# The first normalization of a four-layer graph network in ten parts, and its constants loaded later

## The chip, the core and the metric

The kernel runs on one core of a Trainium2 chip. The core has a matrix engine (PE, TensorE), a vector engine (DVE), a scalar engine (ACT), GpSimd (POOL), and SyncE (SP), which here only issues transfers. Sixteen DMA engines move the data. The metric is the device time of one execution in microseconds (us), lower is better.

## What is computed

A residual stack of four graph layers over 4096 nodes with 128 features, on one dense 4096 x 4096 matrix `adj` in fp32:

```python
h = maximum(layernorm(x), 0);  x = x + (A/deg) @ h @ W_in + (A.T/deg_t) @ h @ W_out
h = maximum(layernorm(x), 0);  x = x + silu(A @ silu(A @ h @ W1 + b1) @ W1 + b1)
h = maximum(layernorm(x), 0);  x = x + relu(normalized(A + I) @ h @ W2 + b2)
h = maximum(layernorm(x), 0);  x = x + relu(normalized(A + I) @ (h @ W3) + b3)
```

`deg` and `deg_t` are the row sums of A and of its transpose. The change touches the first `layernorm` alone, with the loading of `x`, of the five weights and of the three biases.

## The kernel before

**Tiles.** `adj` and its transpose (both laid out by the host) come in tiles of 128 x 1024 fp32, 512 KB each, 768 in all; the code calls a tile's turn a substep. Tiles 0 to 255 are the first layer's; tile n goes through four steps, each on an engine of its own:

- SP loads it (`load(n)`, L316) into one of ten buffers `raw`. From tile 10 on the load waits until DVE is done with tile n - 10 (L320).
- ACT copies it, rounded to the type fp32r (`hi(n)`, L374), with row sums on the side. From tile 8 on this waits until PE has used tile n - 8: the rounded tiles stand in a ring of eight places, six in `a_hi`/`a_lo` and two, for tiles 6, 7, 14, 15, 22, 23 and so on, in the idle feature buffers `h_hi1`/`h_lo1`. So the rows of these tiles read `h_hi` where the others read `a_hi`, and one can tell which tile a row belongs to.
- DVE subtracts, which gives the rest (`lo(n)`, L515).
- PE does six matmuls of 512 columns (`products`, L732): rounded tile times `h_hi` and times `h_lo` of its block of features (L737, four matmuls), rest times `h_hi` (L741, two). The first four need the rounded tile and the features, the last two the rest as well.

**The first normalization.** The features are 32 blocks of 128 nodes. Before the change they are normalized in eight parts of four blocks. A part takes these steps: DVE takes statistics (`first_stats`, L522 and L526), ACT the square root (`first_std`, L388), DVE the reciprocal and bias (`first_affine`, L532 and L534), ACT four relus (`first_relu`, L407) and the rounding to `h_hi` (`split_hi`, L398), and DVE the rest `h_lo` (`split_lo`, L540). Part 0 stands at the start. The others stand among the tiles: the tables FIRST_STATS and so on (L282 to L286) name after which tile each step of which part is issued.

**Which tile needs which features.** Tiles 0 to 47 use blocks 0 to 7 over and over (six runs of eight tiles). From tile 48 on, 16 tiles use blocks 0 to 7, 16 use blocks 8 to 15, and so on; so block 8 is first needed by tile 64, block 16 by tile 80, block 24 by tile 96, block 28 by tile 100. PE waits for `h_ready` at every fourth block (L810). After each run ACT copies two banks out (`copy_partial`, L426), seven and eight tiles after the run's end.

**What follows.** After tile 111 the first block column is complete. PE multiplies it by the weights (L758, eight small matmuls in two rows of 128 columns each, the first after tile 113); this is the first use of a weight, and it waits for all eight loads of weights and biases. ACT's last two copies of the step, behind tile 118, wait in turn for these products.

**SP's order.** x's first eighth (256 KB), tile 0, x's second eighth, tiles 1 to 9, x's second quarter (512 KB), five weights and three biases (64 KB each; a bias is read once for every partition), then tiles from 10 on, with x's third quarter after tile 16 and its last after tile 32.

Of the kernel before, what the change touches and what calls it, by code (L numbers as in the profile page):

```python
# [5 lines left out]
F32 = mybir.dt.float32  # L6
F32R = mybir.dt.float32r
ALU = mybir.AluOpType
# [7 lines left out]
def build_gnn_stack(nc, x, adj, adj_t, w_in, w_out, w1, b1, w2, b2, w3, b3, out):  # L16
# [22 lines left out]
    with ctx:  # L39
# [181 lines left out]


        def split_n(sweep, q):
            return (sweep + 1) * NQ + q

# [55 lines left out]

        FIRST_STATS = {0: 1, 6: 2, 19: 3, 32: 4, 45: 5, 58: 6, 71: 7}  # L282
        FIRST_STD = {0: 1, 10: 2, 23: 3, 36: 4, 49: 5, 62: 6, 75: 7}
        FIRST_AFFINE = {0: 1, 11: 2, 24: 3, 37: 4, 50: 5, 63: 6, 76: 7}
        FIRST_RELU = {1: 1, 14: 2, 27: 3, 40: 4, 53: 5, 66: 6, 79: 7}
        FIRST_LO = {1: 1, 15: 2, 28: 3, 41: 4, 54: 5, 67: 6, 80: 7}  # L286

# [7 lines left out]
        def done1(at, i):  # L295
            return [q for q in range(NQ - 2) if START1 + SLOT1 * q + at == i]

        def halves(at, s):
# [11 lines left out]
        def _(sp):  # L310
# [17 lines left out]
            for n in range(1, RAWS):  # L328
                load(n)
            load_x(2)  # L330
            for i, w in enumerate((w_in, w_out, w1, w2, w3)):
                sp.dma_start(w_sb[:, i, :], w).then_inc(const_in, 16)  # L332
            for i, b in enumerate((b1, b2, b3)):
                sp.dma_start(b_sb[:, i, :], b.rearrange("(a n) -> a n", a=1).to_broadcast([P, D])).then_inc(const_in, 16)

            for n in range(RAWS, len(substeps)):
                load(n)
                if n in (16, 32):
                    load_x(2 + n // 16)

# [29 lines left out]
        def _(act):  # L370
# [13 lines left out]

            def first_std(q):
                blocks = slice(GB * q, GB * q + GB)
                act.wait_ge(mv0_ready, q + 1)
                act.activation(std0[:, blocks], mv0[:, blocks, 1], ACT.Sqrt, bias=eps_sb[:, 0:1]).then_inc(std0_ready, 1)  # L388
# [11 lines left out]

            def first_relu(q):
                act.wait_ge(bias0_ready, q + 1)
                if q > 0:
                    act.wait_ge(h_ready, split_n(-1, q))
                for b in range(GB):
                    n = GB * q + b
                    last = act.activation(act_raw[:, b * D:(b + 1) * D], x_sb[:, n, :], ACT.Relu,  # L407
                                          bias=bias0[:, n:n + 1], scale=rstd0[:, n:n + 1])
                last.then_inc(act_ready, 1)
                split_hi(-1, q)  # L410

# [46 lines left out]

            first_std(0)
            for n in range(S0):  # L460
                _, kind, d, k, _, _ = seq[n]
                hi(n, (row_part if kind else col_part)[:, k, d:d + 1])
                if n == 0:
                    first_relu(0)
                first_layer(n)
# [37 lines left out]
        def _(dve):  # L503
# [13 lines left out]

            def first_stats(q):
                blocks = range(GB * q, GB * q + GB)
                dve.wait_ge(x_in[q if q < 2 else q // 2 + 1], 16)  # L520
                for b in blocks:
                    last = dve.bn_stats(stats0[:, b, :], x_sb[:, b, :])  # L522
                last.then_inc(stats0_ready, 1)
                dve.wait_ge(stats0_ready, q + 1)
                for b in blocks:
                    last = dve.bn_aggr(mv0[:, b, :], stats0[:, b, :])  # L526
                last.then_inc(mv0_ready, 1)

            def first_affine(q):
                blocks = slice(GB * q, GB * q + GB)  # L530
                dve.wait_ge(std0_ready, q + 1)
                dve.reciprocal(rstd0[:, blocks], std0[:, blocks]).then_inc(rstd0_ready, 1)  # L532
                dve.wait_ge(rstd0_ready, q + 1)
                dve.scalar_tensor_tensor(out=bias0[:, blocks], in0=mv0[:, blocks, 0], scalar=-1.0, in1=rstd0[:, blocks],  # L534
                                         op0=ALU.mult, op1=ALU.mult).then_inc(bias0_ready, 1)

            def split_lo(sweep, q):
# [108 lines left out]
            def first_layer(n):  # L646
                if n in FIRST_LO:
                    split_lo(-1, FIRST_LO[n])
                if n in FIRST_STATS:
# [27 lines left out]

            first_stats(0)
            first_affine(0)
            for n in range(S0):  # L680
                lo(n)
                if n == 0:
                    split_lo(-1, 0)
                first_layer(n)
# [45 lines left out]
        def _(pe):  # L730
# [71 lines left out]
            for n in range(S0):  # L802
                r, _, _, k, first, last = seq[n]
                if first and r >= 3:
                    copied, added = drained(r - 3)
                    pe.wait_ge(part_copied, copied)
                    if added:
                        pe.wait_ge(part_added, added)
                if n <= step_end[0] and k % GB == 0:
                    pe.wait_ge(h_ready, k // GB + 1)  # L810
                products(n, h_hi[0][:, k, :], h_lo[0][:, k, :], run_ps[r % 3], first, last)
                first_layer(n)
# [77 lines left out]
```

## Time and profile before

| | |
|---|---|
| median of 3 runs | 1126.58 us (1125.49 to 1129.52) |
| the profiled execution | 1127.55 us, its span 1125.8 us |
| PE busy | 1106.7 us, 98% of the span |
| DVE, ACT busy | 93%, 81% |
| DMA | 363 GB/s on the mean, 95.5% of the 16 engines' time |

The page sums over the whole span. What the change touches is the first tenth, so the rows further down are taken from stretches of it. Times are from the start of the span. A row of the timeline gives start, duration, engine, line, what is written and read and how often; in brackets stands how long the engine was idle before it, and what ended that.

### The profile page before, as it was taken

To read this page: it belongs to the slowest core of one execution; us is meant where nothing else is said; L and a number is where in the kernel's file an instruction comes from. 1 tells how busy PE (TensorE), PEld (TensorE's weight loads), DVE (VectorE), ACT (ScalarE), POOL (GpSimd) and SP (SyncE) were. 2 spreads that over 40 slices of the span, in tenths; PEclk is the share of its full clock that TensorE was granted. 3 is DMA by queue.
4 is the path that set the end of the run, shared out by engine and by line. 5 is a ranking of instruction groups with operands and counts; after the bars stand their busy time and mean duration, and the time that the engine had idled before them with its cause. 6 is when DMAs were issued, how large, how long until landed. Compare 5 with 4: busy or idle time off the path is not lost.

```text
span 1125.8 us, 14740 instructions
## 1 busy us (share of the span) xinstructions
PE 1106.7 (98%) x5056; PEld 914.0 (81%) x5056; DVE 1047.5 (93%) x1452; ACT 912.6 (81%) x1278; POOL 48.0 (4%) x40
## 2 busy tenths in 40 slices
PE   6999999999999999999999999999999999999998
PEld 4778888888888888888888888888888888788886
DVE  6899997999999999989988999999999999998987
ACT  6999987798888688888887888888778778877774
POOL 0000000000000000000000211111111111100000
PEclk9999999999999999999999999999999999999999
DMA  9999998999999899999999999999999999999992
GB/s 327 402 383 404 404 409 318 344 383 409 376 368 348 300 409 409 409 400 363 342 367 377 348 363 356 357 373 333 400 341 354 364 367 326 338 410 374 383 362 114
DMA packets 113835, 408.36 MB, mean 363 GB/s; under 512 B 12640, under 2 KB 13920, under 8 KB 113760
## 3 DMA queue, kind: packets, MB, share of 16 engines
q1 hardware_dynamic: 113760, 407.42, 95.5%
q8 instruction: 40, 0.66, 0.2%
q14 instruction: 35, 0.29, 0.1%
HBM read 405.27 MB, written 2.10 MB: 362 GB/s over the span
## 4 chain that ended last, share of the span: by engine, by line
PE 79%; DVE 13%; DMA 3%; ACT 2%; issue 2%; SPq 1%; ACTq 0%; DVEq 0%
PE bank L737 50%; PE bank L741 25%; DVE a_lo L516 9%; PE bank L758 3%; DMA raw<-in_adj_t_dram 3%; ACT a_hi L381 1%; DVE stats L547 1%; ACT a_hi L383 1%; DVE h_lo L516 1%; SPq L323 1%; DVE x_sb L611 1%; PE bank L799 0%; SPq L332 0%; DVE h_lo L540 0%; DVE acc L604 0%
## 5 line engine op out<-in xcount | busy, mean ns | idle before, releaser
L516 DVE TENSOR_TENSOR a_lo<-raw,a_hi 128x1024 fp32r<-128x1024 f32 x560 | 658.5, 1218 | 39.1 <-ACT a_hi L381 22.1
L737 PE MATMUL bank<-a_hi,h_hi 128*128 128x512 f32 x1400 | 437.5, 394 | 10.9 <-DVE h_lo L540 10.2
L741 PE MATMUL bank<-a_lo,h_hi 128*128 128x512 f32 x1400 | 434.3, 391 | 2.4 <-DVE a_lo L516 1.7
L381 ACT ACTIVATE a_hi<-raw 128x1024 fp32r<-128x1024 f32 x368 | 376.4, 1055 | 71.4 <-PE bank L741 54.3
L737 PE MATMUL bank<-a_hi,h_lo 128*128 128x512 f32 x1400 | 432.4, 390 | 0.0
L741 PEld LDWEIGHTS bank<-a_lo,h_hi 128*128 128x128 f32 x1400 | 261.7, 188 | 64.4 <-DVE a_lo L516 10.8
L737 PEld LDWEIGHTS bank<-a_hi,h_hi 128*128 128x128 f32 x1400 | 259.1, 188 | 64.1 <-DVE h_lo L540 10.2
L737 PEld LDWEIGHTS bank<-a_hi,h_lo 128*128 128x128 f32 x1400 | 263.4, 188 | 55.6
L383 ACT ACTIVATE a_hi<-raw 128x1024 fp32r<-128x1024 f32 x192 | 201.8, 1054 | 27.2 <-PE bank L741 12.2
L516 DVE TENSOR_TENSOR a_lo<-acc,a_hi 128x1024 fp32r<-128x1024 f32 x144 | 169.9, 1219 | 10.6 <-ACT a_hi L381 9.2
L381 ACT ACTIVATE a_hi<-acc 128x1024 fp32r<-128x1024 f32 x144 | 148.7, 1055 | 28.6 <-PE bank L741 26.9
L516 DVE TENSOR_TENSOR h_lo<-raw,h_hi 128x1024 fp32r<-128x1024 f32 x64 | 76.3, 1217 | 7.7 <-ACT h_hi L383 7.3
L383 ACT ACTIVATE h_hi<-raw 128x1024 fp32r<-128x1024 f32 x64 | 67.4, 1054 | 6.1 <-PE bank L741 2.6
L416 ACT ACTIVATE act_raw<-x_sb,lnbias,lnscale 128x128 f32<-128x128 f32 x96 | 39.6, 484 | 33.0 <-DVE lnbias L575 33.0
L363 POOL TENSOR_TENSOR std<-mv,eps_sb 128x4 f32<-128x4 f32 x16 | 17.4, 1087 | 914.5 <-DVE mv L551 914.5
L737 PE MATMUL bank<-h_hi 128*128 128x512 f32 x128 | 39.7, 391 | 1.4 <-ACT h_hi L383 1.4
L741 PE MATMUL bank<-h_lo,h_hi 128*128 128x512 f32 x128 | 39.9, 393 | 0.1
L737 PE MATMUL bank<-h_hi,h_lo 128*128 128x512 f32 x128 | 39.4, 389 | 0.0
L758 PEld LDWEIGHTS bank<-w_sb,prod_t 128*128 128x128 f32 x280 | 36.6, 191 | 2.7
L758 PE MATMUL bank<-w_sb,prod_t 128*128 128x128 f32 x280 | 36.8, 274 | 0.0
L383 ACT ACTIVATION_READ_ACCUMULATOR a_hi<-raw 128x1 f32 x192 | 35.7, 186 | 0.0
L366 POOL TENSOR_TENSOR rstd<-std,minus_half 128x4 f32<-128x4 f32 x16 | 29.9, 1866 | 1.3
(75 smaller groups left out, 420.9 us busy)
## 6 DMA issues: line engine op xcount, KB each, us to landing
raw<-in_adj_t_dram SPq DMA_DIRECT2D x496, 512.0 KB, 6.9
acc<-in_adj_t_dram SPq DMA_DIRECT2D x144, 512.0 KB, 6.7
raw<-in_adj_dram SPq DMA_DIRECT2D x128, 512.0 KB, 7.0
out_dram<-x_sb SPq DMA_DIRECT2D x7, 256.0 KB, 6.8
x_sb<-in_x_dram SPq DMA_DIRECT2D x3, 512.0 KB, 11.7
x_sb<-in_x_dram SPq DMA_DIRECT2D x2, 256.0 KB, 4.0
out_dram<-x_sb SPq DMA_DIRECT2D x2, 128.0 KB, 1.7
w_sb<-in_L_gnn_W_dram SPq DMA_DIRECT2D x3, 64.0 KB, 10.3
```

The source lines that it names most:

```text
L323: sp.dma_start(sub_raw(n), tile).then_inc(tile_in[raw_place[n]], 16)
L363: pool.tensor_tensor(std[:, :], mv[:, :, 1], eps_sb[:, :].to_broadcast([P, GB]), ALU.add)\
L366: pool.tensor_tensor(rstd[:, :], std[:, :], minus_half[:, :].to_broadcast([P, GB]), ALU.pow)\
L381: act.activation(sub_hi_of(n), sub_raw(n), ACT.Copy).then_inc(sub_hi, 1)
L383: act.activation(sub_hi_of(n), sub_raw(n), ACT.Copy, accum_out=accum).then_inc(sub_hi, 1)
L416: last = act.activation(act_raw[:, b * D:(b + 1) * D], x_sb[:, GB * q + b, :], ACT.Relu, bias=lnbias[:, b:b + 1], scale=lnscale[:, b:b + 1])
L516: dve.tensor_tensor(sub_lo_of(n), sub_raw(n), sub_hi_of(n).bitcast(F32), ALU.subtract).then_inc(sub_lo, 1)
L547: last = dve.bn_stats(stats[:, b, :], x_sb[:, GB * q + b, :])
L611: last = dve.scalar_tensor_tensor(out=x_sb[:, block0 + b, :], in0=z_ps[half][:, b * D:(b + 1) * D], scalar=inv[:, which, half * GB + b:hal ...
L737: pe.matmul(bank[half][:, :], weights, hi_a[:, half * GW:(half + 1) * GW], start=start and weights is hi_w, stop=False)
L741: last = pe.matmul(bank[half][:, :], hi_w, lo_a[:, half * GW:(half + 1) * GW], start=False, stop=stop)
L758: last = pe.matmul(z_ps[half][:, b * D:(b + 1) * D], src[:, b * P:(b + 1) * P], w_sb[:, w, :], start=True, stop=True)
```

## The change

- FIRST lists ten parts instead of eight: the first four have two blocks each, the other six four blocks.
- Parts 0 and 1 are worked out ahead of tile 0's `lo` on DVE; on ACT, part 0 and part 1's square root stand ahead of tile 0's `hi`. Parts 2 and 3 follow among tiles 0 to 4. The later parts stand further apart: their relus after tiles 26, 42, 58, 71, 84 and 97 instead of 14, 27, 40, 53, 66 and 79.
- SP loads x's second quarter after tile 11, its third after tile 36 and its last after tile 62. The weights follow after tiles 72, 75, 78, 81 and 84, the biases after 87, 90 and 93.
- PE waits for the features at each part's first block, also at blocks 2 and 6.

```diff
--- before.py
+++ after.py
@@ -220,8 +220,11 @@
+
+        FIRST = [(b, b + GB // 2) for b in range(0, CB, GB // 2)] + [(GB * q, GB * q + GB) for q in range(2, NQ)]
+
         def split_n(sweep, q):
-            return (sweep + 1) * NQ + q
+            return len(FIRST) + sweep * NQ + q
...
-        FIRST_STATS = {0: 1, 6: 2, 19: 3, 32: 4, 45: 5, 58: 6, 71: 7}
-        FIRST_STD = {0: 1, 10: 2, 23: 3, 36: 4, 49: 5, 62: 6, 75: 7}
-        FIRST_AFFINE = {0: 1, 11: 2, 24: 3, 37: 4, 50: 5, 63: 6, 76: 7}
-        FIRST_RELU = {1: 1, 14: 2, 27: 3, 40: 4, 53: 5, 66: 6, 79: 7}
-        FIRST_LO = {1: 1, 15: 2, 28: 3, 41: 4, 54: 5, 67: 6, 80: 7}
+        FIRST_STATS = {0: 2, 1: 3, 18: 4, 34: 5, 50: 6, 64: 7, 77: 8, 90: 9}
+        FIRST_STD = {1: 2, 2: 3, 22: 4, 38: 5, 54: 6, 68: 7, 81: 8, 94: 9}
+        FIRST_AFFINE = {1: 2, 2: 3, 23: 4, 39: 5, 55: 6, 69: 7, 82: 8, 95: 9}
+        FIRST_RELU = {0: 1, 2: 2, 4: 3, 26: 4, 42: 5, 58: 6, 71: 7, 84: 8, 97: 9}
+        FIRST_LO = {0: 1, 2: 2, 4: 3, 27: 4, 43: 5, 59: 6, 72: 7, 85: 8, 98: 9}
...
+        LOAD_X = {11: 2, 36: 3, 62: 4}
+        LOAD_W = {72 + 3 * i: i for i in range(5)}
+        LOAD_B = {87 + 3 * i: i for i in range(3)}
+
+        def act_blocks(b0, b1):
+            return act_raw[:, :].rearrange("p (b f) -> p b f", b=GB)[:, b0 % GB:b0 % GB + b1 - b0, :]
...
-            load_x(2)
-            for i, w in enumerate((w_in, w_out, w1, w2, w3)):
-                sp.dma_start(w_sb[:, i, :], w).then_inc(const_in, 16)
-            for i, b in enumerate((b1, b2, b3)):
-                sp.dma_start(b_sb[:, i, :], b.rearrange("(a n) -> a n", a=1).to_broadcast([P, D])).then_inc(const_in, 16)
-
+            weights = (w_in, w_out, w1, w2, w3)
+            biases = (b1, b2, b3)
             for n in range(RAWS, len(substeps)):
                 load(n)
-                if n in (16, 32):
-                    load_x(2 + n // 16)
+                if n in LOAD_X:
+                    load_x(LOAD_X[n])
+                if n in LOAD_W:
+                    i = LOAD_W[n]
+                    sp.dma_start(w_sb[:, i, :], weights[i]).then_inc(const_in, 16)
+                if n in LOAD_B:
+                    i = LOAD_B[n]
+                    sp.dma_start(b_sb[:, i, :], biases[i].rearrange("(a n) -> a n", a=1).to_broadcast([P, D]))\
+                      .then_inc(const_in, 16)
...
-            def first_std(q):
-                blocks = slice(GB * q, GB * q + GB)
-                act.wait_ge(mv0_ready, q + 1)
+            def first_std(i):
+                blocks = slice(*FIRST[i])
+                act.wait_ge(mv0_ready, i + 1)
                 act.activation(std0[:, blocks], mv0[:, blocks, 1], ACT.Sqrt, bias=eps_sb[:, 0:1]).then_inc(std0_ready, 1)
...
-            def first_relu(q):
-                act.wait_ge(bias0_ready, q + 1)
-                if q > 0:
-                    act.wait_ge(h_ready, split_n(-1, q))
-                for b in range(GB):
-                    n = GB * q + b
-                    last = act.activation(act_raw[:, b * D:(b + 1) * D], x_sb[:, n, :], ACT.Relu,
+            def first_relu(i):
+                b0, b1 = FIRST[i]
+                act.wait_ge(bias0_ready, i + 1)
+                if i > 0:
+                    act.wait_ge(h_ready, i)
+                for n in range(b0, b1):
+                    last = act.activation(act_raw[:, n % GB * D:(n % GB + 1) * D], x_sb[:, n, :], ACT.Relu,
                                           bias=bias0[:, n:n + 1], scale=rstd0[:, n:n + 1])
                 last.then_inc(act_ready, 1)
-                split_hi(-1, q)
+                act.wait_ge(act_ready, i + 1)
+                act.activation(h_hi[0][:, b0:b1, :], act_blocks(b0, b1), ACT.Copy).then_inc(h_hi_ready, 1)
...
             first_std(0)
+            first_relu(0)
+            first_std(1)
             for n in range(S0):
                 _, kind, d, k, _, _ = seq[n]
                 hi(n, (row_part if kind else col_part)[:, k, d:d + 1])
-                if n == 0:
-                    first_relu(0)
                 first_layer(n)
...
-            def first_stats(q):
-                blocks = range(GB * q, GB * q + GB)
+            def first_stats(i):
+                blocks = range(*FIRST[i])
+                q = FIRST[i][0] // GB
                 dve.wait_ge(x_in[q if q < 2 else q // 2 + 1], 16)
                 for b in blocks:
                     last = dve.bn_stats(stats0[:, b, :], x_sb[:, b, :])
                 last.then_inc(stats0_ready, 1)
-                dve.wait_ge(stats0_ready, q + 1)
+                dve.wait_ge(stats0_ready, i + 1)
                 for b in blocks:
                     last = dve.bn_aggr(mv0[:, b, :], stats0[:, b, :])
                 last.then_inc(mv0_ready, 1)
-            def first_affine(q):
-                blocks = slice(GB * q, GB * q + GB)
-                dve.wait_ge(std0_ready, q + 1)
+            def first_affine(i):
+                blocks = slice(*FIRST[i])
+                dve.wait_ge(std0_ready, i + 1)
                 dve.reciprocal(rstd0[:, blocks], std0[:, blocks]).then_inc(rstd0_ready, 1)
-                dve.wait_ge(rstd0_ready, q + 1)
+                dve.wait_ge(rstd0_ready, i + 1)
                 dve.scalar_tensor_tensor(out=bias0[:, blocks], in0=mv0[:, blocks, 0], scalar=-1.0, in1=rstd0[:, blocks],
                                          op0=ALU.mult, op1=ALU.mult).then_inc(bias0_ready, 1)
+
+            def first_lo(i):
+                b0, b1 = FIRST[i]
+                dve.wait_ge(h_hi_ready, i + 1)
+                dve.tensor_tensor(h_lo[0][:, b0:b1, :], act_blocks(b0, b1), h_hi[0][:, b0:b1, :].bitcast(F32),
+                                  ALU.subtract).then_inc(h_ready, 1)
...
             def first_layer(n):
                 if n in FIRST_LO:
-                    split_lo(-1, FIRST_LO[n])
+                    first_lo(FIRST_LO[n])
                 if n in FIRST_STATS:
                     first_stats(FIRST_STATS[n])
                 if n in FIRST_AFFINE:
@@ -677,10 +699,11 @@
             first_stats(0)
             first_affine(0)
+            first_stats(1)
+            first_affine(1)
+            first_lo(0)
             for n in range(S0):
                 lo(n)
-                if n == 0:
-                    split_lo(-1, 0)
                 first_layer(n)
...
-                if n <= step_end[0] and k % GB == 0:
-                    pe.wait_ge(h_ready, k // GB + 1)
+                if n <= step_end[0]:
+                    for i, (b0, _) in enumerate(FIRST):
+                        if k == b0:
+                            pe.wait_ge(h_ready, i + 1)
                 products(n, h_hi[0][:, k, :], h_lo[0][:, k, :], run_ps[r % 3], first, last)
                 first_layer(n)
```

How this moves the instructions. On ACT at the start of the program (`h_hi0`/`h_lo0` are the first layer's features), before:

```order
L388 ACTIVATE zt<-zt,eps_sb 128x4
L383 ACTIVATE a_hi,col_part<-raw 128x1024
L407 ACTIVATE act_raw<-x_sb,zt 128x128 x4
L398 ACTIVATE h_hi0<-act_raw 128x512
L388 ACTIVATE zt<-zt,eps_sb 128x4
L383 ACTIVATE a_hi,col_part<-raw 128x1024
L407 ACTIVATE act_raw<-x_sb,zt 128x128 x4
L398 ACTIVATE h_hi0<-act_raw 128x512
L383 ACTIVATE a_hi,col_part<-raw 128x1024 x4
```

and after:

```order
L402 ACTIVATE zt<-zt,eps_sb 128x2
L421 ACTIVATE act_raw<-x_sb,zt 128x128 x2
L425 ACTIVATE h_hi0<-act_raw 128x256
L402 ACTIVATE zt<-zt,eps_sb 128x2
L397 ACTIVATE a_hi,col_part<-raw 128x1024
L421 ACTIVATE act_raw<-x_sb,zt 128x128 x2
L425 ACTIVATE h_hi0<-act_raw 128x256
L397 ACTIVATE a_hi,col_part<-raw 128x1024
L402 ACTIVATE zt<-zt,eps_sb 128x2
L397 ACTIVATE a_hi,col_part<-raw 128x1024
L402 ACTIVATE zt<-zt,eps_sb 128x2
L421 ACTIVATE act_raw<-x_sb,zt 128x128 x2
```

The first two blocks' features are made ahead of tile 0's copy, and half parts stand between the tiles that follow. On SP, from x's second quarter to the tiles behind it, before:

```order
L323 DMA raw<-in_adj_t_dram 128x1024 x9
L314 DMA x_sb<-in_x_dram 128x1024
L332 DMA w_sb<-in_L0_gnn_W_in_dram 128x128
L332 DMA w_sb<-in_L0_gnn_W_out_dram 128x128
L332 DMA w_sb<-in_L1_gnn_W_dram 128x128
L332 DMA w_sb<-in_L2_gnn_W_dram 128x128
L332 DMA w_sb<-in_L3_gnn_W_dram 128x128
L334 DMA b_sb<-in_L1_gnn_b_dram 128x128
L334 DMA b_sb<-in_L2_gnn_b_dram 128x128
L334 DMA b_sb<-in_L3_gnn_b_dram 128x128
L323 DMA raw<-in_adj_t_dram 128x1024 x7
```

and after:

```order
L334 DMA raw<-in_adj_t_dram 128x1024 x11
L325 DMA x_sb<-in_x_dram 128x1024
L334 DMA raw<-in_adj_t_dram 128x1024 x12
L334 DMA raw<-in_adj_dram 128x1024 x13
L325 DMA x_sb<-in_x_dram 128x1024
```

Tiles 10 and 11 now stand ahead of x's second quarter, and no weight or bias stands there.

## Rows read from the trace of the kernel before

**Rows 1.** The page: the chain that ended last, by engine.

```profile
PE 79%; DVE 13%; DMA 3%; ACT 2%; issue 2%; SPq 1%; ACTq 0%; DVEq 0%
```

**Rows 2.** Stretches: length, busy of PE, PEld, DVE, ACT, POOL, PEclk, DMA share, GB/s.

```profile
30.00:40.00 10.00, 8.49 (x35) 6.05 (x34) 7.41 (x10) 9.71 (x20) 0.00 (x0) 1.00 1.03 410
...
90.00:160.00 70.00, 70.00 (x310) 57.96 (x309) 69.18 (x80) 66.20 (x127) 0.00 (x0) 1.00 1.03 407
160.00:189.00 29.00, 29.00 (x137) 24.31 (x136) 20.55 (x29) 22.00 (x42) 0.00 (x0) 1.00 0.91 352
189.00:213.00 24.00, 24.00 (x114) 19.83 (x113) 24.00 (x34) 18.83 (x35) 0.00 (x0) 1.00 0.94 334
```

**Rows 3.** Timeline of PE: starts of tiles 0, 2, 6, 7, 10 and 22.

```profile
10.24 1.22 PE L737 MATMUL bank<-a_hi,h_hi 128*128 128x512 f32 x2 [10.24 <-DVE h_lo L540]
...
16.04 0.80 PE L737 MATMUL bank<-a_hi,h_hi 128*128 128x512 f32 x2 [0.31 <-ACT a_hi L383]
...
22.01 0.62 PE L737 MATMUL bank<-h_hi 128*128 128x512 f32 x2
...
23.37 0.62 PE L737 MATMUL bank<-h_hi 128*128 128x512 f32 x2
...
27.96 0.73 PE L737 MATMUL bank<-a_hi,h_hi 128*128 128x512 f32 x2 [0.35 <-ACT a_hi L383]
...
47.46 0.62 PE L737 MATMUL bank<-h_hi 128*128 128x512 f32 x2
```

**Rows 4.** Timeline of PE: the first weight product, behind tile 113.

```profile
174.96 1.05 PE L758 MATMUL bank<-w_sb,prod_t 128*128 128x128 f32 x8
```

**Rows 5.** Timeline of DVE at the start.

```profile
3.58 0.87 DVE L522 BATCH_NORM_STATS2 zt<-x_sb 128x6 f32<-128x128 f32 x4 [3.58 <-DMA x_sb<-in_x_dram]
4.49 0.38 DVE L526 BATCH_NORM_AGGREGATE zt<-zt 128x2 f32<-128x6 f32 x4
...
9.49 0.69 DVE L540 TENSOR_TENSOR h_lo<-act_raw,h_hi 128x512 fp32r<-128x512 f32 x1 [0.97 <-ACT h_hi L398]
```

**Rows 6.** Timeline of ACT at the start: square root, tile 0, relus, rounding, tile 2.

```profile
4.90 0.30 ACT L388 ACTIVATE zt<-zt,eps_sb 128x4 f32<-128x4 f32 x1 [2.68 <-DVE zt L526]
...
6.11 1.06 ACT L383 ACTIVATE a_hi<-raw 128x1024 fp32r<-128x1024 f32 x1 [0.91 <-DMA raw<-in_adj_t_dram]
...
7.17 1.63 ACT L407 ACTIVATE act_raw<-x_sb,zt 128x128 f32<-128x128 f32 x4
...
8.83 0.63 ACT L398 ACTIVATE h_hi<-act_raw 128x512 fp32r<-128x512 f32 x1
...
14.86 1.04 ACT L383 ACTIVATE a_hi<-raw 128x1024 fp32r<-128x1024 f32 x1
```

**Rows 7.** Timeline of ACT: tiles 13 and 14, the relus of part 2, tile 15.

```profile
30.59 1.06 ACT L383 ACTIVATE a_hi<-raw 128x1024 fp32r<-128x1024 f32 x1
...
31.87 1.06 ACT L383 ACTIVATE h_hi<-raw 128x1024 fp32r<-128x1024 f32 x1
...
32.93 1.64 ACT L407 ACTIVATE act_raw<-x_sb,zt 128x128 f32<-128x128 f32 x4
...
35.61 1.05 ACT L383 ACTIVATE h_hi<-raw 128x1024 fp32r<-128x1024 f32 x1
```

**Rows 8.** Issue to landing: tile 1 (the second bias alike), tile 9, the third bias.

```profile
DMA to landing us min/median/max: 7.5/7.5/7.5
...
DMA to landing us min/median/max: 12.4/12.4/12.4
...
DMA to landing us min/median/max: 9.2/9.2/9.2
```

**Rows 9.** The chain in order of time: issue to landing of tiles 10 and 22.

```profile
17.40 9.34 DMA raw<-in_adj_t_dram
...
31.88 12.99 DMA raw<-in_adj_t_dram
```

**Rows 10.** Timeline of ACT behind tile 118: the copy that waits for PE's product.

```profile
176.11 0.60 ACT L426 ACTIVATE prod_t<-bank 128x512 f32<-128x512 f32 x1 [3.82 <-PE bank L758]
```

## The prediction, made before the changed kernel ran

> **What bounds the kernel now.** I read the page first: PE's work makes up 79% of the chain that ended last [rows 1]. Then the stretches [rows 2]: from 90 to 160 us PE is busy without a gap, it lacks 1.5 us between 30 and 40, and it has not begun before 10.24 [rows 3]. So PE is the bound once it runs, and the first layer's beginning is worth what PE loses there. A ledger puts a number on that. A tile costs PE 1.36 us (tiles 6 and 7 start at 22.01 and 23.37 [rows 3]); I call *lag* the start of tile n less 1.36 n. It is 10.24 us at tile 0, 13.85 at tile 6 (22.01 - 8.16), 14.36 at tile 10, 17.54 at tile 22 [rows 3], and 19.92 at the marker: the first weight product starts at 174.96 behind 114 tiles, which are 155.04 us [rows 4]. Since PE has no gap from 90 us on [rows 2], it is lost by then. All the change can win lies in these 19.92 us.
>
> **What the five steps of the ledger are.** Up to tile 0, 10.24 us: PE waits for the last step of part 0, DVE's `h_lo` [rows 3, 5]. Tiles 0 to 5, 3.6 us: matmuls at half pace (a pair takes 1.22 us at tile 0 and 0.62 at tile 6) and ACT's second group of relus, behind which tile 2's copy starts only at 14.86 [rows 6]. Tile 10, 0.5 us ahead of its first half (14.36 - 13.85) and about as much ahead of its second: its load is issued at 17.40, behind eight small loads, and lands 9.34 us later [rows 9]. Tiles 11 to 21, 2.7 us (17.54 - 14.85): ACT has just received tile 14 (31.87, with 1.28 us from tile to tile) and then does part 2's relus, so that tile 15 is copied at 35.61 [rows 7]. Tile 22 to the marker, 2.4 us (19.92 - 17.54): the same at the next parts, with smaller amounts since tiles are by then in stock.
>
> **The start (gain 2.5 us at tile 0).** x lands at 3.58 as before. Statistics of two blocks: half of the four take 0.5 and 0.25 us [rows 5], end 4.35. Square root 0.30 [rows 6], reciprocal and bias 0.38 with their gaps, end 5.08. Two relus at 0.4 each plus a fixed 0.1 [rows 6]: 5.96. The rounding of 256 columns: 1024 take 1.06 and 512 take 0.63 [rows 6], so 0.42, end 6.42. Part 1's square root then costs 0.2 more, and tile 0's copy starts at 6.53 (it landed by 6.11 [rows 6], so it is now 0.4 later than before). PE starts 1.18 behind a copy (16.04 - 14.86 [rows 3, 6]): **7.71 instead of 10.24**. DVE's queue: part 1's affine step waits for ACT's square root until 6.65, part 0's `h_lo` follows by 7.38, tile 0's `lo` starts at 7.71; nothing PE needs is behind that wait.
>
> **Tiles 1 to 5 (1 us of it is given back).** I carried the four queues forward with the same durations. ACT has tile 1 at 9.61 (issued at 2.11, it lands 7.5 later [rows 8]; 0.35 us of wait for PE), tile 2 at 11.16, then part 2's square root and relus, which wait for DVE until 12.94, so tile 3 is copied at 14.16, and PE starts it at 15.34 after 0.6 us of wait, and waits 0.2 us for its rest. Part 3's relus put tile 5's copy at 17.46 and its rest at 19.86: 0.5 us more. Tile 6 starts at 20.49 instead of 22.01: **lag 12.33 instead of 13.85**. That the slow matmuls may last into tile 2 or 3 changes nothing up to there: ACT sets the pace.
>
> **Tiles 6 to 26 (all of the next 3.7 us stays away).** The stream of transfers is a queue at 1.28 us a tile [rows 7]. Tile 9 lands at 7.68 + 12.4 = 20.1 [rows 8]. Before, tile 10 came at 26.74 [rows 9]; x's quarter and tile 10 itself explain 2.56 us of the 6.66, so the eight small loads took 4.1. Now tile 10 comes at 21.4, tile 11 at 22.6, x's quarter at 23.9, tile 12 at 25.2, four us sooner, while PE wants tile 12 at 12.33 + 16.3 = 28.6. With part 4's relus only behind tile 26 and x's third quarter behind 36, no wait arises before tile 27. The 1.0 and 2.7 us are gone.
>
> **Tiles 27 to 47.** Tile 22 landed 1.5 us late in the trace (31.88 + 12.99 = 44.87, against 31.87 + nine transfers of 1.28 = 43.4 [rows 7, 9]); I keep that. Tile 26 is then copied at 44.9, relus and rounding take 2.2 us, and tile 27 at 48.1 is ready for PE at 49.3, its rest later still: 1.2 us of wait over two tiles. The parts behind it meet a larger stock (one every 13 to 16 tiles instead of 13, and ACT needs 1.04 us a tile against PE's 1.36), so I count none for them up to tile 72. Before, this stretch cost 2.4. Lag 13.5 instead of 19.92.
>
> **Tiles 72 to 111.** What was taken out of the beginning has to be moved here, where ACT copies tiles almost as they land. By bytes eight loads are 0.52 MB, 1.3 us at 407 GB/s [rows 2]; the whole stretch lost 4.1 us to them. I take 3.2, nearer to what it lost. Parts 8 and 9 then cost PE 0.7 us at tiles 86 to 99. At 1.3 us nothing changes (the stream lags PE no further); at 4.1 it is 0.9 more. With 0.2 us for starts after waits: **lag at the marker 14.4 +- 1, a gain of 5.5 us**; I take 5.4.
>
> The Trainium skill weighs against this place: DMA: Bandwidth & Descriptors, in the part on bandwidth, gives 0.95 us of DMA time for one load of 64 KB and the rule to batch transfers. By it the eight would be 7.6 us and the gain some 1.5 us; the trace had them in 4.1 us, from one burst, which no row shows for loads scattered among tiles.
>
> **Whether the gain lasts.** PE runs 5.4 us nearer to the stream at tile 111. Behind tile 118 ACT waits 3.82 us for PE's product anyway [rows 10], so ACT, DVE and the loads behind them follow PE and move with it. The stream must deliver those tiles sooner: it moved 352 and 334 GB/s in 160 to 213 us where it can do 407 [rows 2], which is 4.0 + 4.4 = 8.4 us to spare. The gain fits. Everything later is bound to PE and shifts.
>
> **The sum.** The profiled execution took 1127.55 us, 1.75 more than its span of 1125.8 and 1.0 above the median; 5.4 less is 1122.2 for it, and 1121.2 against the median of 1126.58. An effect of 0.5% is 5.6 us (1120.95), about what a measurement of this kernel can tell from no change; the forecast lies just inside.
>
> **Rivals.** *The late transfer does not recur:* tile 22 in time, and with it no 1.2 us at tile 27. It happened once in the first fifty tiles of one trace; the gain is then 6.7, time 1119.9. *The small loads stop the stream for longer among tiles than in a burst:* 1 us each instead of 0.5 (4.1 us over eight). The stream is then 4.8 us later at tile 93 than I have it, PE's stock of some 1 us covers little, gain 1.3, time 1125.3. The Trainium skill's figure above comes to about the same. *The gain is taken back behind tile 113*, since the stock before the extra vector work is smaller: against it speaks ACT's wait of 3.8 us; for it, DVE is busy 24.0 of 24 us in 189 to 213 [rows 2]. About half would go: 1124. *Slower than before:* the biases show what a small load can do. The third, issued at 16.30, landed 9.2 us later at 25.5, 2.8 us behind the second (15.20 + 7.5 = 22.7) [rows 8]. If each of the eight holds the stream for 2.8 us between tiles, that is 22 us instead of 3.2, and with little stock PE waits for nearly all of the difference: 13 us lost net, 1140. The point where it decides: above 1.1 us each the gain is gone, above 1.8 us the kernel is slower by 0.5%. Against it: the stream went on moving tiles while that bias came in (tile 10 landed only 1.3 us behind it, at 26.74 [rows 9]), so its 2.8 us were shared.
>
> **How the numbers follow.** Forecast (gain 4.2 to 6.3) 0.63, rival of the early tile 22 0.14, small loads at 1 us 0.10, taken back 0.08, slower 0.05. Range 1119.3 to 1125.3: it takes in the two nearest rivals and the bounds of 1.3 and 4.1 us. Faster by over 0.5%: the first rival and some two fifths of the forecast's own width, 0.40. Within: 0.55. Slower by over 0.5%: 0.05.
>
> **What would show it.** PE's first matmul at 7.7 us; tile 6 at 20.5; no wait for a load at tile 10; tile 27 with 1.2 us of waits; the first weight product at 169.5. If the product comes at 169.5 and the end is not 5 us earlier, the step "whether it lasts" is wrong; if tiles 86 to 100 show more than 1 us of waits, the price of the small loads is.

## The result and the profile after

| | before | changed |
|---|---|---|
| median | 1126.57 us (6 runs, 1125.49 to 1129.52) | 1121.34 us (6 runs, 1120.20 to 1121.92) |
| ratio | | 0.995, 95% interval 0.994 to 0.996 |
| span of the profiled execution | 1125.8 us | 1120.1 us (time 1121.92) |
| first weight product | 174.96 | 169.38 |

The changed kernel is faster by 5.2 us; 1121.2 was forecast. PE's timeline of the changed kernel answers to [rows 3, 4]: the starts of tiles 0, 1, 2, 3 and 6, the last matmuls of tiles 27 and 28, those of tile 99, and the first weight product:

```profile
7.87 1.19 PE L760 MATMUL bank<-a_hi,h_hi 128*128 128x512 f32 x2 [7.87 <-ACT a_hi L397]
...
11.24 1.22 PE L760 MATMUL bank<-a_hi,h_hi 128*128 128x512 f32 x2 [0.47 <-ACT a_hi L397]
...
13.90 0.62 PE L760 MATMUL bank<-a_hi,h_hi 128*128 128x512 f32 x2
...
15.82 0.73 PE L760 MATMUL bank<-a_hi,h_hi 128*128 128x512 f32 x2 [0.39 <-ACT a_hi L397]
...
20.94 0.63 PE L760 MATMUL bank<-h_hi 128*128 128x512 f32 x2
...
50.87 0.73 PE L764 MATMUL bank<-a_lo,h_hi 128*128 128x512 f32 x2
...
52.61 0.73 PE L764 MATMUL bank<-a_lo,h_hi 128*128 128x512 f32 x2
...
149.71 0.74 PE L764 MATMUL bank<-a_lo,h_hi 128*128 128x512 f32 x2
...
169.38 1.05 PE L781 MATMUL bank<-w_sb,prod_t 128*128 128x128 f32 x8
```

PE starts 2.4 us sooner than before and at tile 6 is 1.1 us ahead (20.94 against 22.01). From tile 6 to 26 it never waits (the lag stays at 12.8), where it lost 3.7 us before. ACT and DVE around tile 12 and tile 27 in the changed kernel:

```profile
25.39 1.06 ACT L397 ACTIVATE a_hi<-raw 128x1024 fp32r<-128x1024 f32 x1
...
45.17 1.05 ACT L397 ACTIVATE a_hi<-raw 128x1024 fp32r<-128x1024 f32 x1
...
46.21 1.64 ACT L421 ACTIVATE act_raw<-x_sb,zt 128x128 f32<-128x128 f32 x4
...
48.42 1.04 ACT L397 ACTIVATE a_hi<-raw 128x1024 fp32r<-128x1024 f32 x1
...
49.59 1.22 DVE L531 TENSOR_TENSOR a_lo<-raw,a_hi 128x1024 fp32r<-128x1024 f32 x1 [1.83 <-ACT a_hi L397]
```

Tile 10 was issued at 9.01 (before: 17.40) and landed at 21.53 (before: 26.74 [rows 9]). Part 4's relus at 46.21 put tile 27's copy at 48.42, its rest ends at 50.8, and PE's last matmuls of the tile start at 50.87: waits of 0.55 and 0.38 us at tiles 27 and 28. Later ones are 0.19 at tile 44 and 0.28 at tile 99. Stretches, as in [rows 2]:

```profile
30.00:40.00 10.00, 10.00 (x45) 8.26 (x44) 8.91 (x16) 7.82 (x16) 0.00 (x0) 1.00 1.03 408
90.00:160.00 70.00, 70.00 (x309) 57.51 (x308) 65.68 (x87) 64.77 (x128) 0.00 (x0) 1.00 1.02 396
160.00:189.00 29.00, 29.00 (x138) 24.18 (x137) 25.29 (x38) 24.40 (x47) 0.00 (x0) 1.00 0.99 376
189.00:213.00 24.00, 24.00 (x115) 19.98 (x114) 23.97 (x37) 18.32 (x33) 0.00 (x0) 1.00 0.96 345
```

PE's 1.5 us of idle time between 30 and 40 us are gone. Behind tile 113 the transfers run faster than before (376 and 345 GB/s for 352 and 334), and PE's lead is kept: from tile 130 to tile 767 the changed kernel is 5.5 to 5.6 us ahead throughout. The chain of the page hardly differs:

```profile
PE 79%; DVE 14%; ACT 3%; issue 2%; DMA 2%; SPq 0%; ACTq 0%; DVEq 0%
```

### The profile page after: what moved, and what is told of

It reads as the page before. It is cut to its first block, busy times and chain, and to the rows that moved or that the text cites. A ratio compares the mean times of both kernels' runs of the same rounds, so it can differ in the third digit from the quotient of the medians.

```text
span 1120.1 us, 14768 instructions
## 1 busy us (share of the span) xinstructions
PE 1104.8 (99%) x5056; PEld 914.7 (82%) x5056; DVE 1047.0 (93%) x1458; ACT 912.6 (81%) x1282; POOL 48.0 (4%) x40
## 4 chain that ended last, share of the span: by engine, by line
PE 79%; DVE 14%; ACT 3%; issue 2%; DMA 2%; SPq 0%; ACTq 0%; DVEq 0%
PE bank L760 50%; PE bank L764 25%; DVE a_lo L531 10%; PE bank L781 3%; DMA raw<-in_adj_t_dram 2%; ACT a_hi L395 1%; ACT a_hi L397 1%; DVE stats L569 1%; DVE x_sb L633 1%; DVE h_lo L531 1%; PE bank L822 0%; DVE acc L626 0%; DVE h_lo L562 0%; PE bank L771 0%; DVE mv L573 0%
```

## The experiments

Each is told by its edit, the text on record, and three numbers: landing of tile 10, start of the first weight product (*product*), and the median time with its ratio to executions of the kernel before taken beside it. Landing and product come from one profiled execution, which can lie some tenths of a microsecond, up to 1 us, off the run's median time. The changed kernel itself, measured once more beside the others, shows how far the numbers repeat.

> The changed kernel once more, beside the two that follow, for its time and its ledger in a second execution. The first product should come within 0.5 us of 169.4 and the time within 0.7 us of 1121.3; where it does not, single traces cannot tell differences of half a microsecond.

Measured: 1121.43 us, ratio 0.9958 (0.9943 to 0.9973); tile 10 at 21.35, product 169.02; waits 0.38, 0.38, 0.17 and 0.27 at tiles 27, 28, 44 and 99. Both came as expected. The two products of one kernel differ by 0.4 us, so differences of that size in single traces say nothing.

**One half of the change: the parts alone.** The weights, biases and x's quarters stay where they stood before.

```diff
-        LOAD_X = {11: 2, 36: 3, 62: 4}
-        LOAD_W = {72 + 3 * i: i for i in range(5)}
-        LOAD_B = {87 + 3 * i: i for i in range(3)}
+        LOAD_X = {16: 3, 32: 4}
+        LOAD_W = {}
+        LOAD_B = {}
...
+            load_x(2)
+            for i, w in enumerate(weights):
+                sp.dma_start(w_sb[:, i, :], w).then_inc(const_in, 16)
+            for i, b in enumerate(biases):
+                sp.dma_start(b_sb[:, i, :], b.rearrange("(a n) -> a n", a=1).to_broadcast([P, D])).then_inc(const_in, 16)
```

> The ten parts and their new places alone; x's quarters, weights and biases are loaded at the old places. Theory 1 (the stream of transfers decides, and the half parts' gain at the start is only a wait brought forward): tile 0 starts at 7.8 us, tile 6 near 21.0, but tile 10 still lands at about 26.7 and PE waits there for all it had won, and part 4's relus behind tile 26 cost as much as part 2's did at tile 14; the first weight product comes at 174.8 to 175.0, time 1126.5, no gain. Theory 2 (the terms of the prediction add): the start's 1.1 to 1.5 us and the rarer parts' 1 us stay, the product comes at 172.5 to 173.5 and the time is 1124 to 1125.

Measured: 1126.26 us, ratio 1.0001 (0.9991 to 1.0010), no gain; tile 10 at 27.38, product 173.50. ACT and PE at tile 10:

```profile
27.41 1.06 ACT L402 ACTIVATE a_hi<-raw 128x1024 fp32r<-128x1024 f32 x1 [3.83 <-DMA raw<-in_adj_t_dram]
```

```profile
28.70 0.70 PE L765 MATMUL bank<-a_hi,h_hi 128*128 128x512 f32 x2 [1.79 <-ACT a_hi L402]
```

PE starts as early as in the changed kernel (7.70) and then waits 2.32 us at tiles 10 and 11 (0.98 before), since tile 10 lands no sooner. In the trace 1.5 us are left at the product, between the two theories' numbers. But tile 22, 1.5 us late in the trace of the kernel before [rows 9], came in time in this one, so the 1.5 us cannot be put down to the parts; the times show none of it.

**The other half: the small loads alone.** The kernel before, with its eight parts, and only the eight small loads moved among tiles 72 to 93.

```diff
-            for i, w in enumerate((w_in, w_out, w1, w2, w3)):
-                sp.dma_start(w_sb[:, i, :], w).then_inc(const_in, 16)
-            for i, b in enumerate((b1, b2, b3)):
-                sp.dma_start(b_sb[:, i, :], b.rearrange("(a n) -> a n", a=1).to_broadcast([P, D])).then_inc(const_in, 16)
...
+                if n in LOAD_W:
+                    i = LOAD_W[n]
+                    sp.dma_start(w_sb[:, i, :], (w_in, w_out, w1, w2, w3)[i]).then_inc(const_in, 16)
```

> The kernel before with the five weights and three biases moved behind tiles 72 to 93, and nothing else. Theory 1 (the eight small loads at the start held the stream for 4.1 us, and late they cost next to nothing): tile 10 lands at about 22.6, the product comes at 170.5 to 171.5, time 1122.5. Theory 2 (terms add, and the moved x quarters and rarer parts hold half of the rest): product at 172 to 173, time 1124.

Measured: 1122.46 us (4 runs), ratio 0.9960 (0.9945 to 0.9975); tile 10 at 22.85, product 169.36. The time is theory 1's; the product came 1.1 us sooner than that theory had it. PE of this kernel:

```profile
10.14 1.22 PE L743 MATMUL bank<-a_hi,h_hi 128*128 128x512 f32 x2 [10.14 <-DVE h_lo L546]
...
15.95 0.74 PE L743 MATMUL bank<-a_hi,h_hi 128*128 128x512 f32 x2 [1.17 <-ACT a_hi L389]
```

It starts at 10.14, as late as before, and has its product at the same moment as the changed kernel (169.38). After tile 2 PE waits only at tiles 42 (0.25) and 46 (0.23). In these two traces the changed kernel's earlier start is lost again on the way: 2.3 us ahead at tile 0, 0.9 at tile 6, nothing behind tile 99. The two traces are not quite alike, though. This one is from the fastest of its four executions (1121.64, 0.8 us below the median), and it has no late transfer near tile 22, where the changed kernel's has one. By the medians the changed kernel is 1.0 to 1.1 us ahead (1121.34 and 1121.43), and the intervals of the ratios overlap. So moving the small loads brings most of the gain, 3.7 us by the medians taken side by side and 4.5 by the ratio, and the rest of the change brings between nothing and 1 us.

**The changed kernel with eight whole parts,** part 0 where it stood before, the later ones and all loads as in the change.

```diff
-        FIRST = [(b, b + GB // 2) for b in range(0, CB, GB // 2)] + [(GB * q, GB * q + GB) for q in range(2, NQ)]
+        FIRST = [(GB * q, GB * q + GB) for q in range(NQ)]
...
-        FIRST_RELU = {0: 1, 2: 2, 4: 3, 26: 4, 42: 5, 58: 6, 71: 7, 84: 8, 97: 9}
+        FIRST_RELU = {1: 1, 26: 2, 42: 3, 58: 4, 71: 5, 84: 6, 97: 7}
```

> The changed kernel with eight parts of four blocks: the start is as before the change, the later parts and all loads are as changed. Theory 1 (what the start wins is absorbed by the wait behind tile 26): tile 0 at 10.2, tile 6 at 22.0, no wait at tiles 27 and 28 since more tiles are in stock, product at 169.4 to 169.7, time 1121.3 as with the change. Theory 2 (terms add): 1.0 us of the start is lost to the end, product at 170.4, time 1122.4.

Measured: 1121.97 us, ratio 0.9954 (0.9937 to 0.9970); tile 10 at 21.44, product 168.81, no wait of PE from tile 3 to the product. The product came 0.6 us sooner than theory 1 had it, the time between the two theories; the ratio is that of the changed kernel. By the product the late start has cost nothing against the changed kernel's two traces (169.38, 169.02), and 0.5 us against the trace with ten parts and no late transfer (168.28, the biases in a row below). At the end this execution's span is that of the changed kernel (1120.2): 0.6 us of its lead went between tiles 250 and 270, where the second layer begins; one trace, not followed further.

**The changed kernel with x's quarters at their old places** (after tiles 9, 16 and 32).

```diff
-        LOAD_X = {11: 2, 36: 3, 62: 4}
+        LOAD_X = {16: 3, 32: 4}
...
+            load_x(2)
```

> The changed kernel with x's second, third and last quarter loaded after tiles 9, 16 and 32 as before the change. Theory 1 (the stream decides where tiles are scarce: x's third quarter now stands ahead of tile 27's stock): the waits at tiles 27 and 28 grow by 1.0 to 1.3 us, product at 170.4 to 170.8, time 1122.5. Theory 2 (the quarters' places do not matter, as PE wants tile 12 only at 28.6 us): product at 169.4, time 1121.3.

Measured: 1122.51 us, ratio 0.9964 (0.9952 to 0.9977); product 170.48, 1.3 us behind the changed kernel's two traces (169.38, 169.02). PE waits 0.25, 0.20 and 0.16 at tiles 20, 23 and 24, 1.18 at tile 27 and 0.38 at tile 28:

```profile
50.70 0.73 PE L761 MATMUL bank<-a_hi,h_hi 128*128 128x512 f32 x2 [0.56 <-ACT a_hi L398]
```

A quarter is one tile's bytes; each one that is in the stream ahead of tile 27 puts that tile one transfer later.

**The price of a small load among tiles.** All eight twice, the second copies into a buffer that nothing uses until the first block column is complete (two waits then count sixteen loads; they are left out of the cut):

```diff
                     sp.dma_start(w_sb[:, i, :], weights[i]).then_inc(const_in, 16)
+                    sp.dma_start(prod_t[:, i // 4, i % 4 * D:(i % 4 + 1) * D], weights[i]).then_inc(const_in, 16)
...
+                    sp.dma_start(prod_t[:, 1, (i + 1) * D:(i + 2) * D], biases[i].rearrange("(a n) -> a n", a=1).to_broadcast([P, D]))\
+                      .then_inc(const_in, 16)
```

> The changed kernel with each of the eight small loads issued a second time, into a buffer that is not in use there: sixteen instead of eight behind tiles 72 to 93. Theory 1 (a small load among tiles costs the stream its bytes and little more, 0.2 us): tile 96 lands some 1.5 to 1.8 us later than 138.9, PE's stock covers nearly all of it, product at 169.4 to 169.9, time 1121.5. Theory 2 (the prediction's 0.4 us each): tile 96 3.2 us later, product 2 us later, 1123.5. Theory 3 (0.95 us each): product at 175 or later, time above 1127.

Measured: 1124.21 us, ratio 0.9978 (0.9969 to 0.9987); product 171.93. From one landing to the next the stream takes 1.28 us, and 1.43 to 1.49 where one small load stands between (eight places in each of the changed kernel's two traces): 0.15 to 0.21 us each. A pair of weights took 0.4, as expected of the cheap theory. But the pairs of biases took 0.5, 2.1 and 2.4 us (0.6 and 1.5 of the second at two successive tiles). ACT of this kernel at tiles 90, 91 and 94, and the stretches of this kernel and of the changed kernel's repeat:

```profile
132.03 1.06 ACT L400 ACTIVATE a_hi<-raw 128x1024 fp32r<-128x1024 f32 x1 [0.67 <-DMA raw<-in_adj_dram]
...
134.83 1.06 ACT L400 ACTIVATE a_hi<-raw 128x1024 fp32r<-128x1024 f32 x1 [1.66 <-DMA raw<-in_adj_dram]
...
141.02 1.06 ACT L400 ACTIVATE h_hi<-raw 128x1024 fp32r<-128x1024 f32 x1 [2.51 <-DMA raw<-in_adj_dram]
```

```profile
128.00:132.00 4.00, 4.00 (x19) 3.13 (x18) 4.00 (x5) 3.35 (x8) 0.00 (x0) 1.00 0.89 270
```

```profile
128.00:132.00 4.00, 4.00 (x20) 3.27 (x19) 3.68 (x4) 4.00 (x9) 0.00 (x0) 1.00 1.01 392
```

The DMA engines moved 270 GB/s and were not even full (share 0.89). That is the held-up stream of the prediction's last rival, from something other than a single small load; the next three runs ask what.

**Only the weights doubled,** the first of the two added lines above.

> The changed kernel with the five weight loads doubled and the biases left single. Theory 1 (the loss with all eight doubled came from the biases): each pair costs 0.4 us, tile 96 lands 1.0 us later than 138.9, product at 169.2 to 169.6, time 1121.5. Theory 2 (the loss is of the number of small loads): a loss of some 1.5 us behind tile 90 as with sixteen.

Measured: 1121.30 us (2 runs), ratio 0.9952; product 168.81; a pair costs 0.41 us (1.69 for 1.28), one 0.34. So doubled weights alone do not hold the stream up. The single bias behind tile 93 took 0.32 us in this trace, the most that one did at its late place.

**The three biases in a row** behind tile 93, and **the five weights in a row** behind tile 72:

```diff
-        LOAD_B = {87 + 3 * i: i for i in range(3)}
+        LOAD_B = {93: (0, 1, 2)}
```

```diff
-        LOAD_W = {72 + 3 * i: i for i in range(5)}
+        LOAD_W = {72: (0, 1, 2, 3, 4)}
```

> The changed kernel with its three bias loads issued one behind the other after tile 93 instead of after 87, 90 and 93. Theory 1 (bias loads, 128 reads of one 512-byte row each, are dear when they come close together, as in the kernel before and where they were doubled): tiles 94 to 97 land 2 to 4 us late against 1.28 us a tile, product 1 us or more later than 169.2. Theory 2 (a small load costs 0.2 us wherever it stands, and the 5 us lost at the doubled biases was something else): tiles 94 to 97 land 0.6 us late, product at 169.2 within 0.4.

> The changed kernel with its five weight loads one behind the other after tile 72. Theory 1 (weights are cheap in a row too, only biases are not): tile 73 lands 1.0 us late, product at 169.2 within 0.4. Theory 2 (any small loads in a burst starve the stream, as the 4.1 us at the start suggested): tiles 73 to 76 land 2 us or more late, and PE waits there.

Measured: 1121.29 us (2 runs), ratio 0.9952, product 168.28, and 1121.59 (3 runs), ratio 0.9957, product 168.47. Tile 94 came 1.84 us behind tile 93, so three biases took 0.56; tile 73 came 2.39 behind tile 72, so five weights took 1.11. Neither a bias as such nor a row of small loads is dear at this place. Both products came a little sooner than the 168.8 to 169.6 expected, and so did that of the doubled weights, by 0.4 us. The stretch with the three biases:

```profile
129.00:134.00 5.00, 5.00 (x24) 4.14 (x23) 5.00 (x6) 5.00 (x11) 0.00 (x0) 1.00 1.04 392
```

**The three biases at the start,** behind tile 9, the weights late as in the change.

```diff
-        LOAD_B = {87 + 3 * i: i for i in range(3)}
+        LOAD_B = {}
...
+            for i, b in enumerate(biases):
+                sp.dma_start(b_sb[:, i, :], b.rearrange("(a n) -> a n", a=1).to_broadcast([P, D])).then_inc(const_in, 16)
```

> The changed kernel with the three biases back at the start, behind tile 9 and ahead of tile 10; x's second quarter stays behind tile 11, the five weights stay behind tiles 72 to 84. In the kernel before, x's quarter and eight small loads stood there, and tile 10 landed at 26.74 us; without any of them it landed at 21.53 (changed kernel) and 21.35 (its repeat), 22.18 in the run with the biases in a row late. So x's quarter (1.28) and the eight small loads (about 4) are the difference, and it is open which of the eight. Theory 1, the biases do it (each partition reads the same 512 bytes; they were issued 1.05 us apart): they cost about 3.2 us here, tile 10 lands at 24.6 to 25.2 us, PE waits 1 us or a little less for it (it wants it at about 27.4 in copied form, so from a landing at 25.0 on), first weight product at 169.5 to 170, time 1121 to 1122. Theory 2, all eight cost alike, half a microsecond each: tile 10 at 22.9 to 23.2, no wait there, product 168.5 to 169.4, time 1121. Theory 3, a small load costs 0.2 us wherever it stands and only the full queue of eight with x's quarter costs more: tile 10 at 21.9 to 22.3, product and time as theory 2.

Measured: 1124.21 us, ratio 0.9974 (0.9962 to 0.9985); tile 9 at 20.31, tile 10 at 24.27, product 172.06. Three biases took 3.96 - 1.28 = 2.7 us, 0.9 each, nearest to theory 1 (3.2). What that theory made of it was missed, the product and the time by over 2 us: PE did not wait at tile 10 but behind it, 0.72, 0.47, 0.28 and 0.23 us at tiles 12, 19, 21 and 23 and 1.22 at 27, the last three of these behind a tile 21 that came 1.7 us late. Some 1 us of the missed time is not this kernel's: the kernel before, taken beside it, had 1127.51 us here. SP's timeline, ACT at tiles 10 and 12, and the stretch:

```profile
9.01 1.63 SPq L344 DMA_DIRECT2D b_sb<-in_L_gnn_b_dram  x3
10.68 2.02 SPq L334 DMA_DIRECT2D raw<-in_adj_t_dram  x2
```

```profile
24.30 1.06 ACT L399 ACTIVATE a_hi<-raw 128x1024 fp32r<-128x1024 f32 x1 [1.16 <-DMA raw<-in_adj_t_dram]
...
28.13 1.06 ACT L399 ACTIVATE a_hi<-raw 128x1024 fp32r<-128x1024 f32 x1 [1.41 <-DMA raw<-in_adj_t_dram]
```

```profile
17.00:22.00 5.00, 4.93 (x19) 3.50 (x20) 4.40 (x5) 4.97 (x11) 0.00 (x0) 1.00 0.83 297
```

Tile 10 was issued at 10.68, 13.6 us before it landed, so SP's issue was not what made it late: the stream itself ran at 297 GB/s with a share of 0.83. In the kernel before it was slower still where its biases came in:

```profile
22.00:24.00 2.00, 2.00 (x10) 1.68 (x9) 1.97 (x8) 1.28 (x4) 0.00 (x0) 1.00 0.66 244
```

There all five weights had landed by 21.28, x's quarter at 21.44, and the biases at 21.72, 22.71 and 25.47; tile 10 followed 1.27 us behind the last. Of its 4.1 us the biases would be 2.7 by this run, and 1.4 would be left for the five weights. That is a difference between two executions; the landings show nearly all of the delay among the biases.

**Sixteen parts of two blocks,** one at every seventh tile from 21 on, run twice; a version that might beat the changed kernel.

```diff
-        FIRST_RELU = {0: 1, 2: 2, 4: 3, 26: 4, 42: 5, 58: 6, 71: 7, 84: 8, 97: 9}
+        FIRST_RELU = {0: 1, 2: 2, 4: 3, 21: 4, 28: 5, 35: 6, 42: 7, 49: 8, 56: 9, 63: 10, 70: 11, 77: 12, 84: 13, 91: 14, 98: 15}
```

> The changed kernel with sixteen parts of two blocks, the relus after tiles 0, 2, 4 and then every seventh from 21 to 98. Theory 1 (the waits at tiles 27, 28, 44 and 99 come from relu groups of 2.2 us that ACT cannot spread): they go, product at 167.7 to 168.2, time 1119.7. Theory 2 (more, smaller instructions cost ACT and DVE as much as the spreading saves): product at 169.4 or later, time 1121.3 or more.

> The version with sixteen parts of two blocks once more: product at 167.9 within 0.5 us, time 1120.3 within 0.7 us, 1 us below the changed kernel's 1121.4.

Measured: 1120.31 us, ratio 0.9941 (0.9926 to 0.9956), product 167.94, no wait behind tile 5; and 1121.09, ratio 0.9947 (0.9933 to 0.9961), product 168.42, with waits of 0.11, 0.11 and 0.10 at tiles 44, 51 and 58. The second run just missed what was expected of it. PE no longer waits at tiles 27, 28 and 99. But the lead over the changed kernel, 0.3 to 1.1 us, is about what the two measurements of this one kernel differ by (0.8), so it is not shown to be faster.

## Why the prediction was right, and where its steps were off

**The start.** Forecast 7.71, measured 7.87 (0.16 later). Tile 6: 20.49 against 20.94. The missed 0.45 us is tile 1's: it was copied at 10.04 instead of 9.61, because it landed 7.9 us after its issue instead of the 7.5 of [rows 8] (8.5 in the trace with the weights doubled: this varies between executions).

**Tiles 6 to 26.** Tile 10 was put at 21.4 and tile 12 at 25.2; they came at 21.53 and 25.37, no wait arose, and the 3.7 us stayed away. The price of the small loads in the old place, 4.1 us by subtraction, held (3.9 us sooner in the run with the small loads alone), and the run with the biases alone there shows where most of it lies.

**Tile 27.** The late transfer recurred, at tile 21: 2.95 us behind tile 20, 1.67 more than the usual 1.28. The waits were 0.93 us in place of 1.2. It is not a property of the program: it is there, with 0.9 to 1.7 us at tile 20, 21 or 22, in the trace of the kernel before, in both of the changed kernel, with x's quarters at their old places, with whole parts, with the weights in a row, with the biases at the start and in the second of sixteen parts; it is not in the parts alone, the small loads alone, the doubled small loads, the biases in a row and the first of sixteen parts, and only 0.3 us with the weights doubled. So it stayed away in six of fourteen traces, where the prediction gave that rival 0.14; that it recurred in the changed kernel's profiled execution was partly luck. Where it stayed away with ten parts (doubled small loads, biases in a row, weights doubled), tiles 27 and 28 showed no wait; with the biases in a row the product came at 168.28. That is the first rival's mechanism, worth 0.7 to 1.1 us at the product and not the 1.2 counted.

**Small loads among tiles: the mis-sized term.** Forecast 3.2 us for eight and 0.7 of wait at tiles 86 to 99; measured 0.15 to 0.21 us each, 1.5 in all, and a wait of 0.28. The prediction took its value near the 4.1 us of the burst; the bound by bytes (1.3 us) was the nearer one. The rival at 1 us each falls. The Trainium skill's figure for a 64 KB load, 0.95 us (DMA: Bandwidth & Descriptors, Bandwidth), is measured there on loads issued from GpSimd; as a price per load in this stream, issued from SP, it falls with the rival: no run here shows 0.95 us for a weight, at any place. Only the biases at the start came to 0.9, and late in a row they were 0.19. The rival with 2.8 us each falls as well, though the doubled biases show that its mechanism, a stream held up with tiles in line, exists: 1.7 and 2.0 us above the price of two cheap loads at two places, and 2.8 us of time.

**The sum.** Product 169.5 forecast, 169.38 measured; gain 5.4, measured 5.58 at the product and 5.6 at the end of the span. That the product is within 0.1 us is partly luck, for two errors cancel: tile 1's 0.45 us late, and 0.5 us less of waits at tiles 27 and behind. **Whether it lasts:** ACT's first copy behind tile 118 still waits for PE's product, 1.65 us in place of the 3.82 of [rows 10], and the second as long as before (1.99). The stream ran 24 and 11 GB/s faster, as that step needed. Its 8.4 us to spare are 8.2 by [rows 2]; nothing hangs on the difference.

**What the ledger did not tell.** It was right as a sum, but its terms are not the worth of the edits. The start was booked as 2.5 us (1.5 at tile 6) and the stream as 3.7; the halves of the change, run alone, brought nothing (ratio 1.0001) and some 4 us (ratio 0.9960) in time, and the whole 4.7 to 5.6 (0.9958 and 0.9950). Both are limits on the same PE: what a late start costs is no loss if the stream would make PE wait later on anyway, and what is won at the start is a wait at tile 10 if the stream has not moved. The prediction had x's quarters within the stream's term; they are worth 1.3 us at the product, 1.1 in time.

**What stays open.** Why three biases cost 2.7 us at the start and 0.6 late, and the doubled second and third biases 1.7 and 2.0 us more than two cheap loads. A longer queue is an obvious suspect and does not suffice. The tiles behind the dear ones took long from issue to landing (13.6 us for tile 10 with the biases at the start; 12.6 and 14.8 for tiles 91 and 94 with all doubled; 8.3 for tile 94 with three biases in a row), but these times contain the delay itself. Counted from issues and landings, the dear biases of these two runs were issued behind 7.5 to 9.1 tiles' worth of bytes still under way and the cheap row of biases behind 6.1 to 7.0. Yet with all doubled the pair of weights behind tile 81 and the first pair of biases had 8.4 to 8.5 ahead of them and cost 0.4 and 0.5 us, and the dear biases of the kernel before had only 4.9 to 6.6. In the dear stretches nearly all packets of 512 bytes took 27 ns as elsewhere. A few took up to 0.9 us with the biases at the start, but in the kernel before, where the eight loads cost 4.1 us, only one took over 0.1 us. The cause was not tried by itself, and neither was that of the late transfer.

## What to carry over

Loads that the start does not need belong behind the point where the engines have a stock of tiles: eight transfers of 64 KB cost 4.1 us in the first burst and 1.5 us later, and the engine that bounds the kernel, PE, waited for most of the former. Before an earlier start is built, look at the first wait behind it: here the next limit, tile 10's landing, took back all of it that the times can show, and the simple half of the change (the loads moved) brought some 4 of the 5.2 us. A ledger of where an engine lost time adds up, but what one edit is worth needs that edit alone on the chip.

## What the chip showed that was not expected

- A single 64 KB load among 512 KB tiles, late in the first layer, takes 0.15 to 0.21 us of the stream (0.32 once), close to its share of bytes (0.16 us at 407 GB/s), in 128 packets of 512 bytes.
- The same bias load takes 0.9 us in the first burst; the DMA engines then stand idle for part of the time (share 0.83 at 297 GB/s, and 0.66 at 244 GB/s in the kernel before) with tiles in line.
- Issuing a bias took SP 1.05 us in the kernel before (3.25 us for the three with their gaps), 0.45 to 0.57 in the run with the biases at the start and mostly 0.43 late. So the same issue takes longer or shorter by where it stands; what decides was not tried.
- A transfer of 512 KB came 0.9 to 1.7 us late at tile 20, 21 or 22 in eight of fourteen traces; with sixteen parts it did so in one execution and not in the other of the same kernel.
